# A two-layer graph kernel: edge slots numbered per tile of 128 target rows instead of over the whole graph

## What is computed

```python
agg = jnp.einsum('ij,jh,ijh->ih', adj, node_features, T)
gi = agg @ w_ih.T + b_ih
gh = node_features @ w_hh.T + b_hh
r = jax.nn.sigmoid(ir + hr)
z = jax.nn.sigmoid(iz + hz)
nn_ = jnp.tanh(in_ + r * hn)
return (1.0 - z) * nn_ + z * node_features
...
energy = jax.nn.leaky_relu(s_src[:, :, None] + s_dst[:, None, :], negative_slope=0.2)
energy = jnp.where(adj[None] > 0, energy, NEG_INF)
attention = jax.nn.softmax(energy, axis=-1)
h_prime = jnp.einsum('hij,hjd->hid', attention, h)
...
x = _layernorm(x + _L0_gnn_ref(x, adj, ...), axis=-1)
x = _layernorm(x + _L1_gnn_ref(x, adj, ...), axis=-1)
```

## Time and profile before

| | us |
|---|---|
| three runs | 96.44, 98.01, 97.79 |
| median | 97.79 |
| span of the profiled execution | 96.9 |
| PE busy | 63.4 (547 matmul records) |
| DVE busy | 66.0 (206) |
| ACT busy | 26.0 (66) |
| POOL busy | 26.8 (36) |

### The profile page before, as it was taken

The page is one execution under the profiler, slowest core; times in us unless marked ns, Lnnn a source line. Parts: engine busy times, 40 slices in busy tenths (PEclk is TensorE's granted clock), DMA queues, the critical chain, the costliest instruction groups (busy, mean ns, idle before and its releaser), DMA issues.

```text
span 96.9 us, 1525 instructions
## 1 busy us (share of the span) xinstructions
PE 63.4 (65%) x547; PEld 46.7 (48%) x547; DVE 66.0 (68%) x206; ACT 26.0 (27%) x66; POOL 26.8 (28%) x36
## 2 busy tenths in 40 slices
...
...
GB/s 42 314 250 235 2 0 0 0 0 3 0 27 47 46 49 54 27 52 41 15 7 3 0 0 0 0 10 0 7 0 0 0 0 0 7 0 0 0 0 108
DMA packets 3882, 3.26 MB, mean 34 GB/s; under 512 B 1225, under 2 KB 3026, under 8 KB 3874
## 3 DMA queue, kind: packets, MB, share of 16 engines
...
q0 software_dynamic: 416, 0.85, 4.1%
...
q10 hardware_dynamic: 18, 0.01, 0.0%
...
## 4 chain that ended last, share of the span: by engine, by line
issue 38%; DVE 19%; POOL 15%; PE 14%; DMA 7%; ACT 2%; POOLq 1%; DVEq 0%
POOL edge L340 11%; DVE prefix L770 5%; PE ps_t L511 4%; PE ps_gate L635 4%; DMA xg<-in_x,sidx 3%; DVE pos L799 3%; DMA adj_i<-in_adj 3%; POOL xg L346 3%; PE ps_gate L559 3%; PE ps_b L552 2%; DVE is_ge L791 2%; DVE st L912 1%; DVE pos L802 1%; POOLq L51 1%; POOL rstd L361 1%
## 5 line engine op out<-in xcount | busy, mean ns | idle before, releaser
L361 POOL TENSOR_TENSOR rstd<-epsv,mhalf 128x4 f32<-128x4 f32 x2 | 2.1, 1031 | 46.4 <-DVE epsv L919 46.4
L340 POOL DMA_INDIRECT edge<-in_L_gnn_edge_table,eidx x9 | 11.2, 1243 | 11.2 <-DVE eidx L814 8.7
L511 PE MATMUL ps_t<-pos,rowhot 128*128 128x512 f16 x36 | 10.5, 428 | 5.1 <-DVE pos L802 3.7
L552 PE MATMUL ps_b<-rowhotT,eprod 128*128 128x512 f32 x18 | 10.0, 687 | 2.8 <-DVE eprod L847 2.8
L396 ACT ACTIVATE sgn<-ps_t,slot_half 128x511 f16<-128x511 f32 x9 | 6.2, 692 | 11.9 <-PE ps_t L511 11.9
L709 PE MATMUL ps_gate<-h,colhot 128*128 128x128 bf16 x108 | 9.1, 263 | 0.0
L709 PEld LDWEIGHTS ps_gate<-h,colhot 128*128 128x128 f16 x108 | 8.7, 123 | 0.2
L511 PEld LDWEIGHTS ps_t<-pos,rowhot 128*128 128x128 f16 x36 | 3.4, 106 | 9.9 <-DVE pos L802 4.0
L552 PEld LDWEIGHTS ps_b<-rowhotT,eprod 128*128 128x128 f32 x18 | 3.3, 203 | 8.0 <-issue 7.3
L491 PE MATMUL ps_b<-deg_pad,upper 128*128 128x4 f16 x1 | 0.2, 164 | 9.5 <-DVE sums L773 9.5
L737 PE MATMUL ps_t<-prod,adjT 128*128 128x132 bf16 x108 | 6.4, 220 | 0.0
...
## 6 DMA issues: line engine op xcount, KB each, us to landing
...
edge<-in_L_gnn_edge_table,eidx POOLq DMA_INDIRECT x9, 2.8
...
```

The source lines that it names most:

```text
L340: nc.gpsimd.indirect_dma_start(out=edge[:, c], out_offset=None, in_=edge_table, in_offset=bass.IndirectOffsetOnAxis(ap=eidx[:, c:c + 1], a ...
L361: nc.gpsimd.tensor_tensor(rstd[:], epsv[:], mhalf[:], ALU.pow).then_inc(s_rstd, 1)
L511: mm = nc.tensor.matmul(sel_bank[c % 2], rowhot[:, q, c * P:(c + 1) * P], pos[:, q], start=(q == 0), stop=(q == Q - 1))
L552: mm = nc.tensor.matmul(agg_bank, eprod[:, c], rowhotT[:, c], start=(c == 0), stop=(c == NC - 1))
```

## The change

Nearly every function of the sparse way is written anew; the dense way is kept.

- Slots are numbered in each tile by itself: 320 for each tile. `rowhot` of a tile is one comparison, clamp(slot, base, end) == slot (`held_slots`, `row_onehot`). A tile has two chunks of 128 and a tail of 64; the tails of two tiles share a chunk, so there are ten chunks, worked on in `ORDER`.
- Each tile goes through scan, base, one-hots, selection and index by itself, in place of all four. Selection is now with positions as stationary operand: four matmuls of 128 columns for each chunk give column times slot, and one comparison on VectorE gives `colhot` at once. From chunk 2 on ScalarE first evacuates to fp16 (`keep_sel`). The table's row comes from matmuls of one column (`index`) and one cast (`edge_index`).
- x is gathered on PE for all chunks (`source_features`), together with two transposes that give `rowhot` transposed; the four indirect DMAs of x are gone. x is loaded once, on ScalarE's queue and first there. The splits leave GpSimd; biases are added as fp32 rows.
- Aggregation, gates, GRU, norm, transposition, projection and split go by halves of two tiles: `aggregate(0)` and `gates(0)` stand ahead of the x gathers of the second half. x1 is brought to the output's layout by four more transposes (`natural_x1`).
- The logits' scan runs on 16 partitions, 384 wide. Weighted rows stay fp32, and 12 matmuls scatter them.

```diff
+CAP = 320
+NC = 10
+ORDER = (0, 1, 2, 3, 8, 4, 5, 6, 7, 9)
+ON_DVE = (0, 1)
+IDX = ((0,), (1,), (2, 3), (8,), (4, 5), (6, 7), (9,))
+XGROUP = ((0, 1), (2, 3), (8,), (4, 5), (6, 7), (9,))
+PAIRW = 2 * CAP + 64
...
-            pool.wait_ge(s_bias, 48)
-            nc.gpsimd.tensor_tensor(bias4[:, 0:2], bias4[:, 0:2], bias_hh[:], ALU.add).then_inc(s_bsum, 1)
-            pool.wait_ge(s_bhi, 1)
-            nc.gpsimd.tensor_tensor(bias_lo[:], bias4[:], bias3[:], ALU.subtract).then_inc(s_bres, 1)
...
-            nc.gpsimd.tensor_copy(x3[:, 0], x_il[:]).then_inc(s_x3, 1)
...
-            nc.gpsimd.tensor_tensor(xres[:], x_il[:], x3[:, 0], ALU.subtract).then_inc(s_x3, 1)
-            pool.wait_ge(s_x3, 2)
-            nc.gpsimd.tensor_copy(x3[:, 1], xres[:]).then_inc(s_x3, 1)
-            pool.wait_ge(s_x3, 3)
-            nc.gpsimd.tensor_tensor(x3[:, 2], xres[:], x3[:, 1], ALU.subtract).then_inc(s_x3, 1)
...
-                if (b + 1) * B > CPE:
-                    pool.wait_ge(s_sidx, b - CPE // B + 1)
-                    for c in range(max(b * B, CPE), (b + 1) * B):
-                        nc.gpsimd.indirect_dma_start(
-                            out=xg[:, c], out_offset=None, in_=x,
-                            in_offset=bass.IndirectOffsetOnAxis(ap=sidx[:, c:c + 1], axis=0)).then_inc(s_xs[c], 16)
+            for e in range(len(IDX)):
+                pool.wait_ge(s_idx, e + 1)
+                for c in IDX[e]:
+                    nc.gpsimd.indirect_dma_start(
+                        out=edge[:, c], out_offset=None, in_=edge_table,
+                        in_offset=bass.IndirectOffsetOnAxis(ap=eidx[:, c:c + 1], axis=0)).then_inc(s_edge[c], 16)
...
+            act.dma_start(x_il[:], x.rearrange("(p q) h -> p q h", q=Q)).then_inc(s_x, 16)
...
-                    nc.scalar.activation(sgn[:, c % 2, 0:N - 1], sel_bank[c % 2][:, 0:N - 1], ACT.Sign, scale=-1.0,
-                                         bias=slot_half[:, c:c + 1], accum_out=cnt[:, c:c + 1])
-                    nc.scalar.copy(row1[:, c:c + 1], sel_bank[c % 2][:, N - 1:N]).then_inc(s_cnt, 1)
...
+            squares(0)
+            act.wait_ge(s_xres, 1)
+            nc.scalar.copy(x3[:, 1], xres[:]).then_inc(s_xmid, 1)
+            act.wait_ge(s_hhp, 1)
+            nc.scalar.copy(whhT[:].rearrange("h g p -> h (g p)"), bank[0][:, 0:3 * P]).then_inc(s_hhT, 1)
+            keep_sel(2)
+            keep_sel(3)
+            keep_sel(4)
+            act.wait_ge(s_ihp, 1)
+            nc.scalar.copy(wT[:].rearrange("h g p -> h (g p)"), bank[1]).then_inc(s_ihT, 1)
+            squares(1)
+            keep_xr(0)
+            keep_sel(5)
+            keep_sel(6)
+            squares(2)
+            act.wait_ge(s_wap, 1)
+            nc.scalar.copy(wa, bank[1][:, 0:2 * NH]).then_inc(s_wa, 1)
+            keep_xr(1)
+            squares(3)
+            keep_sel(7)
+            keep_sel(8)
+            keep_sel(9)
+            keep_xr(2)
...
-                        mm = nc.tensor.matmul(sel_bank[c % 2], rowhot[:, q, c * P:(c + 1) * P], pos[:, q],
-                                              start=(q == 0), stop=(q == Q - 1))
...
+                    for jb in range(Q):
+                        if c < 8:
+                            at = sel_bank[k % 2][:, jb * P:(jb + 1) * P]
+                            src = rows_at(c)
+                        else:
+                            at = sel_bank[k % 2][:, jb * P + (t % 2) * 64:jb * P + (t % 2) * 64 + 64]
+                            src = tail_slots(t)
+                        mm = nc.tensor.matmul(at, posm[:, t % 2, jb], src, start=True, stop=True)
...
+                for i, c in enumerate(cs):
+                    for jb in range(Q):
+                        for s in range(3):
+                            nc.tensor.matmul(x_bank[k % 2][:, i * P:(i + 1) * P], cols_at(jb, c), x3[:, s, jb],
+                                             start=(jb == 0 and s == 0), stop=(jb == Q - 1 and s == 2))
+                for i in range(2):
+                    at = (len(cs) + i) * P
+                    src = rows_at(cs[i]) if len(cs) == 2 else tail_rows(2 * (cs[0] - 8) + i)
+                    mm = nc.tensor.matmul(x_bank[k % 2][:, at:at + P], src, ident16[:], start=True, stop=True)
...
+            select(0)
+            select(1)
+            base(1)
...
+            index(0)
+            index(1)
...
+            select(2)
+            select(3)
+            select(4)
+            index(2)
+            base(2)
+            index(3)
...
+            select(5)
+            select(6)
+            base(3)
+            source_features(0)
+            index(4)
+            select(7)
+            select(8)
...
+            source_features(1)
...
+            index(5)
+            select(9)
+            hidden_rn(0)
+            index(6)
+            source_features(2)
...
+            hidden_z(0)
+            bias_in(0)
...
-                    nc.vector.tensor_scalar(is_ge[:, q, 0:n], iota_s[:, slots], base[:, q:q + 1], None, ALU.is_ge)
-                    t = nc.vector.tensor_scalar(is_lt[:, q, 0:n], iota_s[:, slots], cum[:, q:q + 1], None, ALU.is_lt)
-                link(t)
-                nc.vector.tensor_tensor(rowhot[:, :, slots], is_ge[:, :, 0:n], is_lt[:, :, 0:n], ALU.mult)\
-                    .then_inc(s_row, end - first)
...
+                nc.vector.scalar_tensor_tensor(posm[:, t % 2], prefix[:, t].rearrange("p (s j) -> p j s", j=Q),
+                                               tot_in[:, 1, t:t + 1], adj_i[:, t].rearrange("p (s j) -> p j s", j=Q),
+                                               ALU.add, ALU.mult).then_inc(s_pos, 1)
...
+                nc.vector.tensor_tensor(rows_of(t), held[:, t % 2], slot0[:], ALU.is_equal).then_inc(s_row, 1)
...
+                nc.vector.tensor_tensor(colhot[:, :, slots_of(c)], src.rearrange("p (j s) -> p j s", j=Q),
+                                        want.unsqueeze(1).broadcast_to([P, Q, P]), ALU.is_equal).then_inc(s_col, 1)
...
+                for k in range(5):
+                    product(k)
+                gated(0)
+                product(5)
+                product(6)
+                mixed(0, link)
+                moments(0, link)
+                product(7)
+                normalise(0)
+                product(8)
+                dve.wait_ge(s_rr, 1)
+                link(nc.vector.tensor_tensor(newrow[:], rrow[:, 1:VS + 2], rrow[:, 0:VS + 1], ALU.not_equal))
+                nc.vector.tensor_scalar(newrow[:], newrow[:], NEG, None, ALU.mult).then_inc(s_new, 1)
+                product(9)
+                gated(1)
+                keep_u(0)
+                mixed(1, link)
+                moments(1, link)
+                split_h_res(0)
+                split_u(0)
+                normalise(1)
+                split_h_lo(0)
+                keep_u(1)
+                split_u(1)
+                split_h_res(1)
...
-                def residue(b):
-                    cs = slice(b * B, (b + 1) * B)
-                    dve.wait_ge(s_vhi, b + 1)
-                    nc.vector.tensor_tensor(vals[:, cs], vals[:, cs], vals3[:, 0, cs], ALU.subtract).then_inc(s_vres, 1)
...
-                def scatter(chunks, tiles):
-                    for c in chunks:
-                        pe.wait_ge(s_v3, c // B + 1)
-                        for q in tiles:
-                            for k in range(3):
-                                mm = nc.tensor.matmul(num_bank[q // 2][:, q % 2], rowhot_num[:, c, q], vals3[:, k, c],
-                                                      start=False, stop=(c == NC - 1 and k == 2), skip_group_check=True)
-                    return mm
+                def scatter(c, t):
+                    return nc.tensor.matmul(num_bank[t // 2][:, t % 2], rT_at(c, t), vals[:, c],
+                                            start=False, stop=False, skip_group_check=True)
+                pe.wait_ge(s_vals, 1)
+                for c in range(4):
+                    scatter(c, c // 2)
+                pe.wait_ge(s_vals, 2)
+                scatter(8, 0)
+                scatter(8, 1).then_inc(s_num, 1)
+                scatter(9, 2)
+                scatter(9, 3)
+                pe.wait_ge(s_vals, 3)
+                for c in range(4, 8):
+                    mm = scatter(c, c // 2)
+                mm.then_inc(s_num, 1)
...
```

1426 lines of the change are left out of this document (774 added, 652 removed).

## The result

| us | kernel before | changed kernel |
|---|---|---|
| runs, median (lowest to highest) | 97.12 (96.28 to 98.01) | 101.80 (100.58 to 102.95) |
| ratio to before, 95% interval | | 1.045 (1.034 to 1.056) |
| profiled span | 96.9 | 100.3 |

The account below looks back on a forecast made before the run. The prediction took a late first index (26 us) and 13 gathers to bound the kernel up to 50.5, then engine hand-overs. Terms +2.9, -2.8, -0.8, -5.9 and 2.0 of remainder gave 93.2 against 97.8; range 88.5 to 98.5.

Parts of the forecast that it names:

- (1): GpSimd's bias and x splits move to other engines, so VectorE's stall of about 4 us goes.
- (3): Four x gathers go; ten edge gathers, last issued near 37, are 8 us off the path and cost nothing.
- (2): Start of the kernel: tile 0 lands at 4.5, its column one-hots end at 9.7, index 0 at 10.2 against 26.
- (4): Program-order hand-overs through tiles 1 to 3: tile 3's one-hots at 32.5, aggregate(0) starts at 40.8.
- (5): TensorE nearly gapless and fast from aggregate(0) to aggregate(1) copied at 53.4, against 50.5 before: 2.9 us lost.
- (6) to (9): Second half's gates to logits 16.0 us, to exp 8.0, to second reciprocal 5.6, then the unchanged end 7.25.
- remainder of 2.0: Added to the summed layout's 90.3 us for what its arithmetic leaves out, giving a profiled span of 92.3.
- R1: Rival, slower: TensorE stays at 1.2 GHz in 41 to 55, 5 us more, so 98, or 101; chance 0.12.
- (7): Logit reduction to exp: shorter scans, filled by gather matmuls, mean rows and x1 copies; 8.0 us against 8.8.
- my sign of being wrong: Forecast wrong if aggregate(0) starts after 44, products wait for edges, or the granted clock is 0.5 through 42 to 55.
- R3: Rival, no change: some 45 single waits on the chain cost 0.1 more each, 4 us, so 97; chance 0.20.

Follow-up runs that it names:

- kernel with more moves: Changed kernel with four reorderings (copies, exponential, x1, load of x), then further ones on ScalarE, TensorE and VectorE: 82.76 us, again 82.27, ratio 0.804 to the kernel before.
- moved copies: Changed kernel with ScalarE's copies of gathered x placed behind its copies of the selected positions of tiles 2 and 3: 95.76 us against 101.8.
- fillers: Changed kernel with 44 unused matmuls of 128 columns put into TensorE's waits around source_features(0), index(4) and source_features(1): 99.53 us against 102.62.

## Why the prediction was wrong

**(1) and (3) held.** The stall of VectorE went, and gathers are off the path: the last was issued at 40.3 (37 forecast), and twice the gathers changed nothing.

**(2) was 1.5 short.** Landing at 5.38 instead of 4.5; the positions instruction took 1.13 in place of 0.6, beyond even my upper bound of 0.9. By base(3) three of them and the landing make 2.5 us, of which forecast and trace show 2.3. The bound went by arithmetic on another instruction's pace; one with two 16- and 32-bit sources in steps had no row.

**(4) had the waits right and their worth wrong.** From base(3) to tile 3's one-hots layout and trace agree within 0.1 (13.4 and 13.3 us), the stalls of 4.2 and 5.1 among them, which I had announced as 3 to 5. I took them for the price of the change. They were mostly the price of two lines' places: moving these gave 6 us, part of it by the faster pace that came with it, the largest effect of any single edit. A layout instruction by instruction shows what an order costs only if each wait is asked what else that engine could do.

**(4), its last terms, and (5) failed on the pace.** My sum has TensorE fast in z and from aggregate(0) on; it was slow up to 52, at a granted clock of 0.50. From 34.7 to aggregate(0) 11.6 us instead of 8.3: z and its bias rows 3.2 instead of 1.3, which I had costed fast (fast they take 1.7 in the kernel with more moves, so 0.4 is mis-sized arithmetic and 1.5 the pace); the empty rows with their copy took 2.0 instead of 1.4, hidden_rn(0) and source_features(2) with index 6 some 0.4 more each. In (5), aggregate(0) with its copy 3.4 instead of 2.0 (the second half's, fast, took 2.0) and gates(0) 2.5 instead of 1.3, both slow (fast, in the kernel with more moves, gates(0) take some 1.5); hidden_later 3.8 instead of 3.1 at the fast pace, bias rows again. Together aggregate(1) was copied at 62.4, 9.0 late: 2.3 of prices, 3.3 ahead of aggregate(0), 3.4 behind it.

**(6) to (9) came out in their sum, and that in part by luck.** To the logits 17.5 instead of 16.0, to exp 9.1 instead of 8.0: 2.6 late. To the reciprocal 4.1 instead of 5.6, 1.5 early, because the scatter ran fast, 0.25 a matmul and not 0.4. The end 7.2, as said. Together 37.9 against 36.9; the remainder of 2.0 that I had added covered this 1.0 and 1.0 of the rest. So the span is late by 9.0 + 1.0 - 2.0 = 8.0 us.

**The rivals.** R1 is what came, in 41 to 52: z 1.5, the empty rows 0.4, aggregate(0) 1.4 and gates(0) 1.0 are over 4 us of slow pace, near its 5. Its own sum gives 98; the rest up to 101.8 are the 2.3 of (2) and the terms mis-sized in (4) to (7). I gave it 0.12, and my sign of being wrong, aggregate(0) behind 44, came true at 46.3. The argument against it, that work is dense from 41 on, was wrong as an argument: work was nearly dense from 35 on (9.62 of 10 us, then 5.87 of 7) and the pace stayed slow for 17 us. The rule of the Trainium skill, page "TensorE: Matmul & The Clock Gate", section "HAM oscillation — how this bites in real kernels", that gaps between bursts bring the low clock back, agrees with the moved copies and the fillers, which removed gaps and won speed in 25 to 37; the fall at 37 in the filled kernel, in work without a gap since 34.1, it does not explain, nor the 17 us of slow pace in nearly dense work. R3, dearer hand-overs in some 45 small waits, was not measured by itself; the waits that experiments took out were few and large.
